# Cross attention with three banks in rotation: where the value projections of the next batch stand in a period

## What is computed

```python
x = x + _L0_attn_ref(_layernorm(x), ...)
x = x + _L0_xattn_ref(_layernorm(x), ctx_1024, wq, bq, wk, bk, wv, bv, wo, bo)
x = x + _L0_ffn_ref(_layernorm(x), gate_w, wg, wu, wd)

def _L0_xattn_ref(query, value, wq, bq, wk, bk, wv, bv, wo, bo):
    q = _split_heads(query @ wq.T + bq, B)        # 16 heads of depth 8
    k = _split_heads(value @ wk.T + bk, B)
    v = _split_heads(value @ wv.T + bv, B)
    scores = jnp.einsum('bhqd,bhkd->bhqk', q, k) / scale
    attn = jax.nn.softmax(scores, axis=-1)
    ctx = jnp.einsum('bhqk,bhkd->bhqd', attn, v)
    return ctx.transpose(0, 2, 1, 3).reshape(B, -1, D_MODEL) @ wo.T + bo
```

## Time and profile before

| what | value |
|---|---|
| device time, median of 3 runs | 625.28 us (624.89 to 627.48) |
| the profiled execution: its own time, and its span | 624.53 us, 622.4 us |
| PE busy | 575.1 us, 92% of the span |
| DVE, ACT, POOL busy | 444.6 us (71%), 377.4 us (61%), 299.6 us (48%) |
| granted TensorE clock, mean over the span | 0.98 of full |

### The profile page before, as it was taken

How to read it: one execution, slowest core, us unless ns; L and a number is a source line. 1 busy time by engine, 2 the same in 40 slices (tenths; PEclk the granted TensorE clock), 3 DMA queues, 4 the chain that set the end, 5 groups by cost and what they waited for, 6 DMA issues and landing times.

```text
span 622.4 us, 17454 instructions
## 1 busy us (share of the span) xinstructions
PE 575.1 (92%) x6584; PEld 475.4 (76%) x6584; DVE 444.6 (71%) x851; ACT 377.4 (61%) x603; POOL 299.6 (48%) x213
## 2 busy tenths in 40 slices
PE   3699686799999999999999999999999989999997
PEld 1466373487888888788788788888888769999985
DVE  4865466776787787777777778678686567766776
ACT  2467545246665765765765665675667676677663
POOL 4585314566547447547546636736320234334430
PEclk9899989789999999999999999999999999999999
DMA  6000005397484385385376376367270102111000
GB/s 221 1 3 3 0 2 121 65 206 186 115 196 103 98 198 111 94 191 122 90 184 131 92 173 142 97 156 148 82 172 3 52 1 89 58 58 51 1 1 34
DMA packets 25430, 59.91 MB, mean 96 GB/s; under 512 B 14120, under 2 KB 14504, under 8 KB 25392
## 3 DMA queue, kind: packets, MB, share of 16 engines
q1 hardware_dynamic: 25392, 59.38, 39.9%
HBM read 20.49 MB, written 0.52 MB: 34 GB/s over the span
## 4 chain that ended last, share of the span: by engine, by line
PE 69%; ACT 7%; issue 3%; DVE 3%; POOL 1%; ACTq 0%; DVEq 0%; POOLq 0%
PE PS L1769 13%; PE PS L1729 13%; PE PS L1753 12%; PE PS L1782 7%; PE PS L1784 7%; PE PS L226 7%; PE PS L1783 6%; ACT k_full L247 3%; ACT k_hi L246 2%; PE PS L1739 1%; ACT P L1296 1%; DVE chunk_max L1455 1%; PE PS L1778 1%; DVE PS L1622 1%; PE PS L1845 1%
## 5 line engine op out<-in xcount | busy, mean ns | idle before, releaser
L1455 DVE TENSOR_REDUCE chunk_max<-PS 128x1 f32<-128x500 f32 x336 | 212.9, 673 | 68.6 <-PE PS L1729 68.5
L1296 ACT ACTIVATE P<-PS 125x896 f32<-125x896 f32 x192 | 174.4, 919 | 132.5 <-PE PS L1753 131.5
L1729 PE MATMUL PS<-k_hi,q_block_hi 128*128 128x500 f32 x336 | 129.5, 436 | 2.7 <-DVE chunk_max L1455 1.2
L256 POOL TENSOR_TENSOR k_lo<-k_full,k_hi 128x500 fp32r<-128x500 f32 x48 | 61.0, 1274 | 130.3 <-ACT k_full L247 128.1
L1753 PE MATMUL PS<-q_stack,k_stack 97*125 97x224 f32 x768 | 121.2, 281 | 1.4 <-ACT P L1296 1.2
L1753 PEld LDWEIGHTS PS<-q_stack,k_stack 97*125 97x125 f32 x768 | 108.9, 190 | 14.8 <-ACT P L1296 5.5
L1769 PE MATMUL PS<-P,values 125*32 125x112 f32 x3072 | 83.6, 260 | 0.7 <-issue 0.7
L1769 PEld LDWEIGHTS PS<-P,values 125*32 125x32 f32 x3072 | 72.0, 110 | 14.9 <-issue 9.5
L1729 PEld LDWEIGHTS PS<-k_hi,q_block_hi 128*128 128x128 f32 x336 | 61.6, 196 | 19.4 <-DVE chunk_max L1455 11.1
L1622 DVE TENSOR_TENSOR PS<-gated,PS 128x448 f32<-128x448 f32 x64 | 40.2, 629 | 30.5 <-PE PS L1784 27.5
L1353 ACT CAST hid_hi<-PS 128x448 fp32r<-128x448 f32 x64 | 34.2, 534 | 36.9 <-DVE PS L1622 36.9
(11 more groups left out here) (202 smaller groups left out, 973.2 us busy)
## 6 DMA issues: line engine op xcount, KB each, us to landing
k_stack<-k_hi SPq DMA_DIRECT2D x128, 187.5 KB, 4.8
ctxT<-ctx_in SPq DMA_DIRECT2D x16, 750.0 KB, 4.4
k_stack<-k_lo SPq DMA_DIRECT2D x64, 187.5 KB, 4.5
w_gate_up<-wgu_in SPq DMA_DIRECT2D x8, 512.0 KB, 3.7
w_down<-wd_in SPq DMA_DIRECT2D x8, 256.0 KB, 3.8
q_stack<-neg_rows SPq DMA_DIRECT2D x112, 0.5 KB, 2.7
q_copies<-q_hi SPq DMA_DIRECT2D x8, 98.0 KB, 4.0
X<-x_in SPq DMA_DIRECT2D x1, 512.0 KB, 3.7
```

The source lines that it names most:

```text
L256: nc.gpsimd.tensor_tensor(k_lo[:, j, k], k_full[:, k], k_hi[:, j, k].bitcast(F32), ALU.subtract).then_inc(k_lo_ready, 1)
L1296: nc.scalar.activation(P[:, t % RING, :].rearrange("p (a n) -> p a n", a=2), PS[0:KR, 2 * (t % 2):2 * (t % 2) + 2, 0:HALF], ACT.Exp).then_ ...
L1455: nc.vector.tensor_reduce(out=chunk_max[:, n // KC, n % KC:n % KC + 1], in_=PS[:, max_bank(b, n), 0:KW], axis=AX.X, op=ALU.max).then_inc(m ...
L1729: nc.tensor.matmul(PS[:, max_bank(b, n), 0:KW], q_block_hi[:, j, 128 * t:128 * t + 128], k_hi[:, j, KW * c:KW * c + KW], start=True, stop= ...
```

## The change

`VALUE_SLOTS = [1, 2, 4]` is gone. `VALUE_PLACES` puts the first value block into slot 2, ahead of the denominators, and the other two into slot 5, behind the first key block and ahead of the second chunk places and of `weigh`. DVE reads them in the same slots. No work is added or taken away.

```diff
-            KEY_SLOTS, VALUE_SLOTS, TURN_SLOTS = [5, 6, 7], [1, 2, 4], [3, 8]
+            KEY_SLOTS, TURN_SLOTS = [5, 6, 7], [3, 8]
+            VALUE_PLACES = {2: [0], 5: [1, 2]}
...
-                    for name, slots in (("key", KEY_SLOTS), ("value", VALUE_SLOTS), ("out", [OUT_SLOT]), ("turn", TURN_SLOTS)):
+                    for name, slots in (("key", KEY_SLOTS), ("out", [OUT_SLOT]), ("turn", TURN_SLOTS)):
                         if t in slots:
                             before.append((name, slots.index(t)))
+                    before += [("value", c) for c in VALUE_PLACES.get(t, [])]
...
-                            if exists(b + 1, B) and t in VALUE_SLOTS:
-                                c = VALUE_SLOTS.index(t)
-                                read_values(dve, b + 1, 1 - j, c, bank("value", c))
+                            if exists(b + 1, B):
+                                for c in VALUE_PLACES.get(t, []):
+                                    read_values(dve, b + 1, 1 - j, c, bank("value", c))
...
-                            if exists(b + 1, B) and t in VALUE_SLOTS:
-                                c = VALUE_SLOTS.index(t)
-                                take_bank(BANK_OF["value", c], (v_ready, KC * (b + 1) + c + 1))
-                                project_values(pe, b + 1, 1 - j, u if j == 0 else u + 1, c, bank("value", c))
+                            if exists(b + 1, B):
+                                for c in VALUE_PLACES.get(t, []):
+                                    take_bank(BANK_OF["value", c], (v_ready, KC * (b + 1) + c + 1))
+                                    project_values(pe, b + 1, 1 - j, u if j == 0 else u + 1, c, bank("value", c))
```

## The result

| | before | after |
|---|---|---|
| device time, median (lowest to highest), 4 runs each | 625.24 us (624.89 to 627.48) | 647.85 us (646.88 to 649.43) |
| ratio after to before, 95% interval | | 1.0356 (1.0324 to 1.0389) |
| span of the profiled execution | 622.4 us | 647.4 us |
| PE busy, share of the span | 575.1 us, 92% | 583.4 us, 90% |

A forecast was written before the change was run, and what follows sets the result against it. The prediction took PE's order of work as the time, with DVE nearly full in slots 1 to 5. 14 periods of 1.39 us less 0.3 made 19.2 us, 644.5 us as a median; range 640 to 649, own bounds 641.8 to 647.

The forecast's parts named there:

- What bounds: Slots 1 to 5: PE's order of work sets the time, but DVE is busy 8.79 of 9.76 us and already late.
- Neighbours worth nothing: Fewer fp32r to plain fp32 changes around value blocks on PE gain zero, 0.6 us at the most over the kernel.
- Slot 2 and slot 4: Denominators behind value0 wait nothing or some 0.05 us; the key block's late bank goes, gaining 0.15 us per period.
- Slot 5: Value1 takes max16's bank, read by DVE only behind both reciprocals and the scaling; each period gets 1.39 us longer.
- The idle time itself: PE idle 1.2 to 1.6 us before a value block in slot 5, some 14 times, 18 to 22 us in all.
- The weight load: Before value1 in slot 5, a load not hidden behind the late bank adds 0.10 us; hidden, 1.4 us less in all.
- Period 14: The period without a key block, where PE already stood idle 0.70 us before `weigh`, was counted as 1.39 us longer too.
- the rival in which the clock falls: PE falls to 1.2 GHz behind 1.6 us idle per period, 48 us on top, 692 us; 4 in 100.
- Period 0: No reciprocals there, so no wait before value1, and a gain of about 0.3 us.
- The loads: SP's next context load comes 1 us later, landing at 280.3, before POOL turns to it at 282.53; covered by 2 us.
- Sum: 14 x 1.39 - 0.3 = 19.2 us on 624.53, giving 643.7; as a median, 644.5 us.

The follow-up runs named there:

- v01_slot2: Against the changed kernel, value0 and value1 in slot 2 and value2 back in slot 4: 626.15 us, ratio 0.9997 to the kernel before.
- v2_slot5: Against the changed kernel, value0 and value1 back in slots 1 and 2, only value2 in slot 5: 647.2 us, ratio 1.0354 to the kernel before.
- v12_behind: Changed kernel with value1 and value2 behind `weigh` of slot 5, not ahead of it: 630.9 us, ratio 1.0092 to the kernel before.
- max16_first: Changed kernel with DVE taking max16 ahead of the second reciprocal and the scaling of slot 4: 641.61 us, ratio 1.023 to the kernel before.
- v2_slot6: Against the changed kernel, value blocks in slots 1, 2 and 6: 623.14 us, ratio 0.9968 to the kernel before; repeated, 624.26 us, ratio 0.9979.
- relieved_b: v1_6_v2_7 with one chunk maximum moved from slot 2 to slot 7: 624.05 us, ratio 0.9967 to the kernel before.
- v1_6_v2_7: Against the changed kernel, value blocks in slots 1, 6 and 7: 623.74 us, ratio 0.9949 to the kernel before.
- gate_later: Changed kernel with ScalarE rounding expert 0's gate and up weights in slots 7 and 9 of period 14, not 4 and 6: 645.64 us, ratio 1.0348.

## Why the prediction was right, and where it was short

- *What bounds.* Right. DVE's chain of slots 1 to 5, 8.79 us of 9.76, was the thing to see, with PE first in the chain that ended last.
- *Neighbours worth nothing.* Right: predicted at most 0.01 us for each change of type, and v01_slot2 gave 0.01 for two, together with a move. The entry into `weigh` behind a value block is paid as before.
- *Slot 2 and slot 4.* Right: the denominators follow value0 without idle time (276.33 to 277.21 is 0.88), and the key block starts 0.23 behind its chunk.
- *Slot 5.* Right in mechanism and in size: value1 at 7.28 us behind the scores of slot 1 (I had 273.97 - 266.74 = 7.23), `weigh` at 9.22 (I had 9.15), the period 1.42 longer (I had 1.39). v2_slot5, v12_behind and max16_first each take the mechanism apart, and each period came out within 0.1 us of the same arithmetic.
- *The idle time itself.* Too large: I gave 1.2 to 1.6 us, 18 to 22 in all, and the view has 1.14, 17.4 in all. The view counts from the modelled end of the last key pass (281.35), my 1.6 from where its successor would have started (280.96 + 0.23 = 281.19), which makes 0.16. And PE came to value1 5.97 us behind the scores of slot 1 (281.19 - 275.22), where my sum had 272.38 - 266.74 = 5.64: I let the transposition and the chunks around it follow without a wait. PE's late start shortens the idle time and leaves the period alone, since DVE sets when it ends.
- *The weight load.* The 0.10 us that I added by the row, against the rule, belongs there: value1, value2 and the entry into `weigh` took 1.94 us, and 0.97 + 0.87 + 0.08 is 1.92. In period 0 of the same trace, where they follow the key block without idle time, they took 1.84 (135.54 to 137.38).
- *Period 14.* **This term was mis-sized**: "I count 1.39 for it too" measured 5.16. The 1.39 is in it, but two parts were missing. The scaling is on the new path, so what lengthens it (GpSimd, 0.87 us) now counts. And the rival in which the clock falls came true in this one period of 14, for 2.9 us. I had held a row of 1.42 us idle at the full clock against it, which says nothing about 2.71. This is read from one execution; whether the clock fell in the others isn't recorded by period.
- *Period 0.* I counted a gain of 0.3 us; it took 0.1 us more. The value blocks did not wait, but the scores of period 1 now waited 0.58 us for the DMA of the row maxima, as the row at 149.97 shows.
- *The loads.* Right, no wait came of them: SP issued the load at 284.70, 4.3 us to landing makes 289.0, and GpSimd turned to it at 292.47.
- *Sum.* 19.2 us forecast from 624.53, 22.6 measured between the medians: short by 3.4, of which period 14 is 3.8. The profiled pair differs by 25.0 in span, of which 1.2 lie ahead of period 0. The start of period 0 varied from 122.9 to 127.3 us over the profiles of this study, with the same code ahead of it, so that part is no effect of the change. That the median stayed in the range has some luck in it: in the profiled executions periods 0 to 14 alone differ by 23.8 us, not 19.2, and the changed kernel's own time there, 649.43 us, is above the range. (The upper bound of the sum, 647, left out the 0.3 of period 0, which the lower one takes off; with it 646.7.)

## What to carry to other kernels

With banks dealt in rotation, moving a product gives it, and everything after it, another predecessor in its bank: look up who reads that one, and what stands ahead of that reader in its own queue, before asking what the product's neighbours are. An engine with 30% of slack over the kernel can have none in the ten microseconds that count; move work to the stretch where the reader is idle, not to where the writer is in the right mode. A new wait must be priced in every variant of the loop body, the written-out last ones too: here 1 period of 14 held more than a fifth of the loss. For the same reason a shorter loop body is not yet a faster kernel: v2_slot6 gained 1.5 us in 13 periods and gave back 1.0 to 1.2 in the two at the ends.

## What the runs showed of the hardware

- A VectorE operation with two inputs in SBUF took 1.26 us, not 0.39, when it started 0.26 us behind a GpSimd operation of 1.27 us that reads SBUF; it ended 0.25 us behind that one's end (476.11 + 1.27 = 477.38, and 476.37 + 1.26 = 477.63). With GpSimd's work elsewhere it took 0.39. In the kernel before it took 0.64, and it also ended 0.25 behind the split (457.20 + 1.27 = 458.47, and 458.08 + 0.64 = 458.72). In relieved_b the order was the other way: the scaling started first (453.70) and took 0.39, and the split started 0.02 later and took 1.52 instead of 1.27. The Trainium skill, SBUF — State Buffer, Who interferes with whom, says that a DVE instruction with two SBUF inputs and a GpSimd instruction that reads SBUF contend, and that the order of issue decides which of them blocks. These traces agree.
- Idle time of PE and the granted clock behind it: the clock stayed at 1.00 behind 1.14 us in the changed kernel, 1.42 us in period 0, 1.86 us in v1_6_v2_7 and 2.10 us in max16_first, and fell to the level of 1.2 GHz behind 1.69 us in relieved_b, 1.84 us in gate_later, 2.70 us in v2_slot5 and 2.71 us with the change. So the length of the idle time alone does not decide; what does, no run here shows. The rows of v1_6_v2_7 (clock 1.00 from 148.71 to 156.00) and of relieved_b (0.61 from 468.00 to 470.00, then 0.54; 64 matmuls of `weigh` take 2.46 us by the view, against 1.74):

```profile
148.71 0.69 PE L1755 MATMUL PS<-q_stack,k_stack 97*125 97x224 f32 x4 [1.86 <-DMA q_stack<-neg_rows]
466.99 0.67 PE L1755 MATMUL PS<-q_stack,k_stack 97*125 97x224 f32 x4 [1.69 <-DMA q_stack<-neg_rows]
467.58 2.46 PE L1771 MATMUL PS<-P,values 125*32 125x112 f32 x64
```

- Going from fp32r to plain fp32 products of full width and back, on TensorE, had no price that a period of 23 us could show (0.01 us for two such changes together with a move of one block).
